# Edge passes of a graph-attention kernel: transposes five tiles ahead, gathers seven ahead, groups of nine tiles, and the running sum placed by its pair

## What is computed

```python
def _gatv2(x, src, dst, Wl, bl, Wr, br, att, bias):
    xl = (x @ Wl + bl).reshape(N, H, C)
    xr = (x @ Wr + br).reshape(N, H, C)
    e = jax.nn.leaky_relu(xl[src] + xr[dst], NEG_SLOPE)
    logits = jnp.einsum('ehc,hc->eh', e, att)
    m = jax.ops.segment_max(logits, dst, num_segments=N)
    p = jnp.exp(logits - m[dst])
    s = jax.ops.segment_sum(p, dst, num_segments=N)
    alpha = p / s[dst]
    out = jax.ops.segment_sum(xl[src] * alpha[..., None], dst, num_segments=N)
    return out.reshape(N, H * C) + bias
...
x = x + gnn(layernorm(x))    # two _gatv2 layers with elu between them, N=20000, H=4, C=128
x = x + ffn(layernorm(x))
```

## Time and profile before

| | us |
|---|---|
| median of 3 runs | 3166.66 (3163.56 to 3170.2) |
| the profiled execution, its own time | 3174.08 |
| its span in the trace | 3172.4 |
| edge pass of layer 0, first gather to last store of the join | 541.6 to 1130 |
| edge pass of layer 1, the same | 1665.9 to 2243 |
| PE, DVE, ACT, POOL busy over the span | 2673.3, 2457.8, 1492.2, 1191.1 |

### The profile page before, as it was taken

The page is one execution under the profiler, slowest core; times in us unless marked ns, Lnnn a source line. Parts: engine busy times, 40 slices in busy tenths (PEclk is TensorE's granted clock), DMA queues, the critical chain, the costliest instruction groups (busy, mean ns, idle before and its releaser), DMA issues. The chain is left out here.

```text
span 3172.4 us, 39733 instructions
## 1 busy us (share of the span) xinstructions
PE 2673.3 (84%) x11179; PEld 1822.6 (57%) x11179; DVE 2457.8 (77%) x5347; ACT 1492.2 (47%) x3619; POOL 1191.1 (38%) x1132
## 2 busy tenths in 40 slices
PE   7999997987776359999998887863399999969997
PEld 5777775433332148888873333331288888846665
DVE  7999996777776647767657778776688888649998
ACT  4545553144443523333321444435478888715554
POOL 0022211566654223333316666552333333104444
PEclk8999998988887679999998989886599999979999
DMA  8989997467775558887755777765799999739999
GB/s 325 341 306 319 317 340 285 147 193 200 200 208 167 156 205 278 274 267 266 263 210 173 206 201 206 200 187 146 286 367 356 349 345 348 238 117 252 249 252 177
DMA packets 320437, 787.02 MB, mean 248 GB/s; under 512 B 53744, under 2 KB 54288, under 8 KB 310010
## 3 DMA queue, kind: packets, MB, share of 16 engines
q1 hardware_dynamic: 220152, 539.68, 48.2%
q0 software_dynamic: 97616, 241.01, 30.8%
q10 hardware_dynamic: 2452, 3.79, 0.3%
HBM read 468.08 MB, written 328.75 MB: 251 GB/s over the span
## 5 line engine op out<-in xcount | busy, mean ns | idle before, releaser
L932 PE MATMUL bank<-wr,nT_e 128*128 128x512 f32 x1264 | 644.7, 658 | 0.0
L1093 PE MATMUL bank<-whi,t_hi 128*128 128x512 f32 x1256 | 524.9, 418 | 23.1 <-DVE t_lo L409 23.1
L1095 PE MATMUL bank<-whi,t_lo 128*128 128x512 f32 x1256 | 499.7, 398 | 0.0
L1094 PE MATMUL bank<-wlo,t_hi 128*128 128x512 f32 x1256 | 498.0, 397 | 0.0
L932 PEld LDWEIGHTS bank<-wr,nT_e 128*128 128x128 f32 x1264 | 259.1, 216 | 275.6 <-issue 275.6
L788 DVE TENSOR_TENSOR z_e<-bank,ring_e 128x1024 f32<-128x1024 f32 x158 | 192.9, 1221 | 237.3 <-issue 201.2
L727 ACT COPY nT_e<-bank 128x512 f32<-128x512 f32 x158 | 92.1, 584 | 527.4 <-PE bank L935 525.9
L924 PE MATMUL bank<-ident,ring_e 128*128 128x128 f32 x632 | 120.1, 320 | 239.1 <-DMA ring_e<-rows,src_row 238.9
L699 POOL TENSOR_TENSOR z_e<-z_e,v_att 128x512 f32<-128x512 f32 x158 | 202.3, 1281 | 289.1 <-DVE z_e L794 288.9
L960 POOL DMA_INDIRECT g_vin<-touched,node_slot x157 | 175.3, 1117 | 320.2 <-DMA g_xin<-in_x 302.4
L960 POOL DMA_INDIRECT vin<-touched,node_slot x157 | 170.7, 1088 | 332.4 <-DMA vin<-rows 314.9
(11 more groups left out here) (242 smaller groups left out, 5834.5 us busy)
## 6 DMA issues: line engine op xcount, KB each, us to landing
rows<-t_row SPq DMA_DIRECT2D x312, 512.0 KB, 3.8
touched<-acc_e SPq DMA_DIRECT2D x158, 256.0 KB, 4.3
xin<-in_x SPq DMA_DIRECT2D x156, 256.0 KB, 4.7
xTin<-in_xT SPq DMA_DIRECT2D x156, 256.0 KB, 3.6
w_e<-w_e POOLq DMA_DIRECT2D x78, 512.0 KB, 4.6
vin<-rows SPq DMA_DIRECT2D x156, 256.0 KB, 4.0
g_vin<-rows SPq DMA_DIRECT2D x156, 256.0 KB, 5.8
g_xin<-in_x SPq DMA_DIRECT2D x156, 256.0 KB, 6.6
```

What stands on the lines that cost most here:

```text
L932: pe.matmul(psR[b][:, :], nT[:, b, cc, :], wr[:, cc, :], start=(cc == 0), stop=False)
L1093: pe.matmul(ps, hi[:, cc, :], whi[:, cc, :], start=(cc == 0), stop=False)
L1094: pe.matmul(ps, hi[:, cc, :], wlo[:, cc, :], start=False, stop=False)
L1095: last = pe.matmul(ps, lo[:, cc, :], whi[:, cc, :], start=False, stop=(cc == KC - 1))
```

## The change

Four things change. PE transposes tile k + 5 in step k, no longer k + 6. POOL gathers tile k + 7, no longer k + 6. Groups have nine tiles, the last two 4 and 3, which makes ten groups. An add is due one step behind the weigh of the second tile of its pair, and the accumulates one and two steps behind the add (`added_at`, `sum_at`). Where one tile is weighed a step, this is `weigh_at + 3` for both tiles of a pair as before; where two are, the first tile of a pair is now accumulated a step earlier than the second. Of the accumulates after the last tile, the last three stand behind the share chain, where one stood before.

```diff
-G = 10
-LAST = (5, 4)
+G = 9
+LAST = (4, 3)
 CATCH = 30
-LEAD = 6
+LEAD = 7
...
-    steps = weigh_at[-1] + 5
-
-    def due(k, at, late):
-        return [t for t in range(T) if at[t] + late == k]
+    added_at = [weigh_at[min(t | 1, T - 1)] + 1 for t in range(T)]
+    sum_at = [added_at[t] + 1 + t % 2 for t in range(T)]
+    steps = sum_at[-1] + 1
+
+    def due(k, at):
+        return [t for t in range(T) if at[t] == k]
...
-        late = [t for t in range(T) if weigh_at[t] + 3 >= T]
+        late = [t for t in range(T) if sum_at[t] >= T]
...
-                for t in due(k, weigh_at, 1):
+                for t in due(k, added_at):
                     add_own(t)
...
-                for t in due(k, weigh_at, 3):
+                for t in due(k, sum_at):
                     accumulate(t)
...
-            for k in range(T, steps - 2):
-                for t in due(k, weigh_at, 3):
-                    accumulate(t)
+            for t in late[:-3]:
+                accumulate(t)
             dve.wait_ge(s["others_loaded"], 16)
...
-            for k in range(steps - 2, steps):
-                for t in due(k, weigh_at, 3):
-                    accumulate(t)
+            for t in late[-3:]:
+                accumulate(t)
...
-            pipeline(T, [(transposes, 6), (roots, 4)])
+            pipeline(T, [(transposes, 5), (roots, 4)])
```

More of the change, by code:

```diff
@@ L749, in _ @@
                     copy_transposed(k + 4)
-                for t in due(k, weigh_at, 0):
+                for t in due(k, weigh_at):
                     weigh(t)
```

## The result

The changed kernel takes 2970.45 us (median of 4 runs, 2969.6 to 2972.14) against 3165.85 (4 runs, 3163.56 to 3170.2): a ratio of 0.9382, 95% interval 0.9366 to 0.9398. That is 195 us less. The forecast was 3000 (a gain of 167), with a range of 2935 to 3095.

A forecast was written before the change was run, and what follows sets the result against it. The prediction took a loop over several engines as the bound. Its terms, 97 + 13 + 4 + 50 + 8 - 5 = 167 us, led from the profiled 3174.1 to 3007, and 3000 us as median; range 2935 to 3095.

The forecast's parts named there:

- The bound and the loop: Middle of a pass: a loop over several engines spans three tiles, 18 to 20 us; the leads spread it over five.
- The middle: Tiles 14 to 60 of each pass: 5.35 us a tile instead of 6.44, giving 97 us over both layers.
- The clock as a rival: PE's clock falls as short waits for banks multiply, taking gain back: 85 us in all, 3082; chance 0.2.
- The floor as a rival: All of DVE's idle time returns, leaving only its own work: 226 us, 2941; chance 0.2.
- DMA: Rival: the DMA engines give no more than a 0.75 share, so a tile takes 6.2 us: 3118; chance 0.05.
- The copy on ACT, the rival on the other side: With one tile of lead, ACT's copy is exposed between transposes and product: about 6.8 us a tile, 3204; chance 0.04.
- The first 14 tiles: Start of each pass, before DVE accumulates: PE's remaining wait for rows all goes, 13 us, bounds 5 and 13.
- The end of the loop: Tiles 60 to 78: the chain of weighs, sums, adds and gathers loosens, 50 of 82 us idle, bounds 20 and 70.
- The share chain: After the last tile: the chain needs tile 75 only and runs beside the last weighs, 4 us a pass, 8.
- One more group: Groups of nine add one group a pass, costing DVE 2.6 us in each: -5.
- The signs: Expected in the profile after: pair_sums at 4.7 in runs of six or more, share chain over before tile 78's add.

The follow-up runs named there:

- e3: The kernel before with transposes at +5 alone, gathers still at +6: 2983.98 us, ratio 0.945.
- e10: The kernel before with transposes at +5, groups of ten, sums placed by pair and the attention vector of DVE's product in PSUM; gathers at +6: 2951.28 us.
- e4: The changed kernel with groups of ten, 5 and 4 at the end, keeping both leads and the sums placed by pair: 2968.65 us.
- e8: The changed kernel with only the last accumulate behind the share chain, not the last three: 2971.37 us.
- e6: The changed kernel with DVE's product right behind leaky, ahead of logits and pair_sums: 2958.36 us.
- e5: The changed kernel with the attention vector of DVE's product in a spare PSUM bank: 2951.09 us.
- e9: The kernel before with both leads, groups of ten, sums placed by pair and the attention vector of DVE's product in PSUM: 2950.05 us.

## Why the prediction was right, and where its sizes were off

**The bound and the loop.** "The pace is set by a loop over several engines" was right, and so was the mechanism: PE's wait for rows in the middle went from 57.3 to 0.9 us, and e1, which changes the two leads only, has 182 of the 195 us. One step was more than was needed: the prediction spread "18 us to 20 us" over the five tiles that both leads give, while over the four tiles that either single lead gives they are 4.5 to 5 us a tile, already under DVE's pace. e3 fits that, with 5.15.

**The middle.** 5.35 us a tile was forecast and 5.23 measured, 108 us instead of 97 - 5. That these lie close is partly luck, since 5.35 was taken from PE's time, and it is DVE that sets the pace. The two reasons given for staying above DVE's floor were both mis-sized, in opposite directions. PE does not keep its present low clock: it is at 0.98 in the middle, and PE needs 220.1 / 46 = 4.79 us a tile, not 5.21. And the "floor" of 4.93 is not DVE's floor: in the changed kernel DVE is busy for 239.4 / 46 = 5.20. Of the 12.6 us more, 11.9 are one line, the product, 43.3 us at a mean of 940 ns instead of 31.4 at 682 (46 each); the rest is the balance of one more group in the stretch and small differences. In the kernel before DVE was idle for a quarter of the time, and a busy time read in that state holds only what the engine meets in it. In e10, with groups of ten and no long product, DVE is busy for 226.7 us over the same 46 tiles, 4.93 a tile again, at a pace of 5.11.

**The clock as a rival** (chance 0.2) did not come. PE waits for banks in 16 tiles, 19.9 us, none longer than 2.5, and is at 2.4 GHz nearly all the time (0.98). The Trainium skill's observation on cycling through PSUM banks ("TensorE: Matmul & The Clock Gate", "A second HAM failure mode: psum-queue depth-cycling") would have had it swing; by that, the trace disagrees, with 0.98.

**The floor as a rival** (0.2, 2941) was right that DVE's waits for the product bank in the middle go altogether, 71.1 us to none. It still missed by 29 us: DVE's work grew at the same time, by 12.6 us in the middle of layer 0 alone, and the share chain gave nothing.

**DMA**: the share rose from 0.72 to 0.89, as it would have to (0.87 forecast), and PE waited 0.9 us for rows. The copy on ACT, the rival on the other side, shows as 10 waits, 17.9 us in all, of PE's weight loads, with no wait left on DVE. That rival's 6.0 us divides the copy on ACT by PE's clock too; with 0.5 + 4.0 alone over 0.87 it is 5.9, which changes nothing.

**The first 14 tiles** gave 14.5 us, with 13 as the upper bound: PE, busy 64.8 of 72 us before, is busy 63 of 63, with the clock at 1.00 instead of 0.98.

**The end of the loop**: 50 us were forecast, with bounds of 20 and 70; 76 came. The chain of the earlier trace rows is gone: PE's wait for rows of 40.1 us in layer 0 is at none, POOL's for weighs went from 32.3 to 4.2 us. But the bounds assumed that some idle of DVE would stay, and there is hardly any (98.1 busy of 99.5). ACT, whose 5.3 us a step were the reason to give back 50 only, is busy for 54.2 of the 99.5: by the tables 6 of the 19 steps in which DVE adds up the pairs of tiles 60 to 78 (57 to 75) have no weigh at all. The term was too low. Its account is also incomplete: it put the tables first, and the leads alone give 57 of the 76 us (e1), the placing by pair 4 more (e4) and the groups of nine 14.5, which they lose again behind tile 78 but for about 1 us.

**The share chain**: 8 us were forecast, none came. The step that failed is "the end moves from 1116.0 to about 1112". The chain does start earlier, 37.5 us behind tile 78's `pair_sums` instead of 39.5, but no more than that: it waits for the add of tiles 74 and 75, and the weigh of tile 75 began only after DVE had summed tile 69, behind its work on the trails. Groups of nine also let the last weigh end 1.4 us later, and three sums behind the chain take 2.9 us where one took 0.8. The timeline of DVE at the chain's start:

```profile
996.37 1.64 DVE L853 SCALAR_TENSOR_TENSOR acc_e<-acc_e,same,w_e 128x512 f32<-128x512 f32 x2 [6.31 <-DMA w_e<-w_e]
997.92 1.07 DVE L887 TENSOR_TENSOR z_e<-z_e,joins 128x512 f32<-128x512 f32 x1
```

So the last sum of layer 0 ends 47.1 us behind tile 78, where it ended at 47.0. e8 sizes the placing at 0.7 us a pass. The same placing with groups of ten, e4, does move the end, by 6.9 and 6.1 us against e1, most of it through the weighs, the last of which ends 4.5 us earlier.

**One more group**: 5 us were forecast for both passes, 4.2 measured in the middle (2.2 and 2.0), and given back elsewhere.

**The signs.** Most came, but two did not. `pair_sums` follow at 4.7 in runs of four at most, not six or more, as the long products stand between them. And the share chain is over 44.2 us behind tile 78, 4 us after tile 78's add has landed, not before.

## What to carry to other kernels

When a loop of waits runs through several engines, count how many tiles it spans and divide its length by them: in this kernel one more tile of distance at one place was enough, as the quotient was then near or below the fullest engine's own work, and more distance bought nothing. Price the fullest engine not by its busy time in the old kernel but with the collisions that a full engine will meet. Of two engines that can hold each other up, order the work so that the one with spare time is the one that waits (12 us in e6), or give the other an input in another memory (19 us in e5), and then look which instruction is met instead.

## What the hardware showed that I had not expected

DVE's 128x512 product of two SBUF operands takes 0.68 us alone. Held up by POOL's product of two SBUF operands, it ends 0.56 us behind POOL's end: 1.85 to 1.90 us where the two start within 0.05 us. An accumulate is held up the same way, to 1.3 us in most cases of e9 and e10 and to 2.58 in a few, where it even started 0.7 us ahead of POOL's product. POOL's product takes 1.27 us alone and up to 1.78 where it is the one that waits, in e6. Which one waits is not settled by the recorded starts. With one operand in PSUM the DVE product never exceeded 0.686 us in 158 (e5), at the same speed otherwise. PE's clock held at 0.98 through a stretch in which PE was busy for 220 of 241 us, with 16 waits of up to 2.5 us.
